# Layer 0's first twelve units: the second product in one piece, behind both pairs of scores and in front of the second tile for the maximum

## The reference, cut to what matters

```python
q = (x @ Wq.T + bq).reshape(b, s, NHEADS, DK)       # 16 heads, width 8, s = 2048
k = (x @ Wk.T + bk).reshape(b, s, NHEADS, DK)
v = (x @ Wv.T + bv).reshape(b, s, NHEADS, DV)
w = jnp.einsum('bshd,bzhd->bhsz', q, k)
w = w / jnp.sqrt(jnp.float32(DV))
w = jax.nn.softmax(w, axis=-1)
vw = jnp.einsum('bhsz,bzhd->bshd', w, v)
out = vw.reshape(b, s, NHEADS * DV) @ Wo.T + bo
```

## Time and profile before

| | us |
|---|---|
| median of 3 runs | 1083.95 (1082.78 to 1086.41) |
| the profiled execution, device time | 1085.42 |
| its span in the profile | 1083.6 |
| PE busy | 1007.7 (93%) |
| DVE busy | 900.6 (83%) |
| ACT busy | 824.1 (76%) |
| POOL busy | 195.8 (18%) |
| mean granted TensorE clock | 0.972 of 2.4 GHz |

### The profile page before, as it was taken

How to read it: one execution, slowest core, us unless ns; L and a number is a source line. 1 busy time by engine, 2 the same in 40 slices (tenths; PEclk the granted TensorE clock), 3 DMA queues, 4 the chain that set the end, 5 groups by cost and what they waited for, 6 DMA issues and landing times.

```text
span 1083.6 us, 22172 instructions
## 1 busy us (share of the span) xinstructions
PE 1007.7 (93%) x8654; PEld 341.6 (32%) x8654; DVE 900.6 (83%) x1153; ACT 824.1 (76%) x1584; POOL 195.8 (18%) x370
## 2 busy tenths in 40 slices
PE   6889999999999999999998899999989998899997
PEld 2422222222222222222232244334344563323323
DVE  8989999999999999999988677766778767897604
ACT  4149999998999998999986577666755676656785
POOL 4533200003000003000024200231042113110112
PEclk9569999999999999999999899999999999999997
DMA  3820511000000000000001441115200431200000
GB/s 98 204 79 7 141 32 26 6 2 2 2 2 2 3 2 2 2 1 3 2 2 31 144 129 51 40 32 94 35 2 9 141 106 37 34 10 1 1 11 11
DMA packets 46422, 41.68 MB, mean 38 GB/s; under 512 B 5598, under 2 KB 44478, under 8 KB 46318
## 3 DMA queue, kind: packets, MB, share of 16 engines
q1 hardware_dynamic: 44062, 34.87, 13.1%
q0 software_dynamic: 1824, 5.25, 1.7%
q10 hardware_dynamic: 432, 0.13, 0.0%
HBM read 26.44 MB, written 13.30 MB: 37 GB/s over the span
## 4 chain that ended last, share of the span: by engine, by line
PE 71%; DVE 13%; ACT 8%; issue 4%; DMA 1%; POOL 1%; another core or an unknown queue 1%; SPq 0%; POOLq 0%; ACTq 0%; DVEq 0%
PE O L989 26%; PE T L957 14%; PE S L917 9%; DVE mx L1280 8%; ACT PT L1527 4%; PE S L924 4%; PE T L966 3%; PE S L1102 2%; PE S L1068 1%; ACT PT L1521 1%; PE S L1058 1%; PE T L1110 1%; PE S L966 1%; PE T L998 1%; PE T L1090 1%
## 5 line engine op out<-in xcount | busy, mean ns | idle before, releaser
L1280 DVE TENSOR_REDUCE mx<-S 128x2 f32<-128x1024 f32 (+2 forms) x672 | 759.3, 1180 | 72.4 <-PE S L917 25.3
L1527 ACT ACTIVATE PT<-T 128x512 f32<-128x512 f32 (+2 forms) x1280 | 675.8, 580 | 116.5 <-PE T L966 49.4
L989 PE MATMUL O<-PT,Va 128*9 128x256 f32 (+1 forms) x4032 | 317.7, 387 | 3.3 <-ACT Os L1562 3.3
L917 PE MATMUL S<-Ks,Qs 48*128 48x512 bf16 x1024 | 205.5, 394 | 12.1 <-DVE mx L1280 9.6
L957 PE MATMUL T<-Qs,Ks 51*128 51x512 bf16 x1024 | 202.0, 387 | 13.4 <-ACT PT L1527 9.3
L957 PEld LDWEIGHTS T<-Qs,Ks 51*128 51x128 bf16 x1024 | 56.2, 93 | 224.1 <-issue 126.7
L989 PEld LDWEIGHTS O<-PT,Va 128*9 128x9 f32 x4032 | 59.8, 88 | 207.1 <-issue 197.5
L924 PE MATMUL S<-K,Qs 96*128 96x512 bf16 (+3 forms) x320 | 89.4, 349 | 5.3 <-DVE mx L1280 4.9
L966 PE MATMUL T<-Qs,K 99*128 99x512 bf16 (+3 forms) x256 | 67.4, 344 | 11.9 <-ACT PT L1527 8.3
L989 PE MATMUL O<-PT,V 128*17 128x512 f32 (+3 forms) x616 | 72.5, 540 | 0.0
L917 PEld LDWEIGHTS S<-Ks,Qs 48*128 48x128 bf16 x1024 | 52.4, 95 | 34.7 <-DVE mx L1280 27.3
(11 more groups left out here) (303 smaller groups left out, 815.3 us busy)
## 6 DMA issues: line engine op xcount, KB each, us to landing
Qs<-in_L_ffn_experts SPq DMA_DIRECT2D x28, 192.0 KB, 2.4
Ks<-in_L_ffn_experts SPq DMA_DIRECT2D x20, 192.0 KB, 2.6
Vf<-sorted_x SPq DMA_DIRECT2D x12, 256.0 KB, 4.8
sorted_y<-Vf SPq DMA_DIRECT2D x12, 256.0 KB, 2.3
Qs<-rows_q SPq DMA_DIRECT2D x24, 128.0 KB, 4.5
rows_q<-q SPq DMA_DIRECT2D x7, 384.0 KB, 2.5
Qs<-rows_q SPq DMA_DIRECT2D x36, 64.0 KB
sorted_x<-XP POOLq DMA_DIRECT2D x1, 1792.0 KB, 10.7
```

Source lines behind the costliest of these rows:

```text
L917: m = e.matmul(two[:, i, :], Qs[r0:r0 + 48, hp, q0:q0 + 128], Ks[r0:r0 + 48, hp, CH * kb:CH * kb + CH], start=True, stop=True, tile_positi ...
L989: m = e.matmul(acc[32 * g:32 * g + d1, lo:hi], v, PT[(2 * j + g // 2) % 4][:, p0 + lo:p0 + hi], start=fresh, stop=True, skip_group_check=n ...
L1280: e.tensor_reduce(mx[:, u % 2, h0:h0 + 2, kb], two[:, :, 0:n], AX.X, ALU.max).then_inc(free, 1)
L1527: e.activation(PT[(2 * j + pair) % 4][:, CH * i + lo:CH * i + CH], bank[:, lo:CH], ACT.Exp).then_inc(free, 1)
```

## The change

In the layer 0 branch of the step loop, for units 0 to 11 (`u < 12`, with u the unit of the scores), the first half of the product is no longer emitted behind the first tile for the maximum, nor the second at the end of the step. The whole product is emitted in one piece right behind the second pair of scores, and the remaining k - 1 tiles for the maximum come behind it. Units 12 to 15 and layer 1 are as before.

```diff
@@ -524,13 +524,18 @@
         emit_st(J, 0)
         if L == 0 and k:
             emit_s()
-            emit_pv(J - LAG, (0,))
+            if u >= 12:
+                emit_pv(J - LAG, (0,))
             do_light(0.5)
             do_later()
             emit_st(J, 1)
+            if u < 12:
+
+                emit_pv(J - LAG, (0, 1))
             for _ in range(k - 1):
                 emit_s()
-            emit_pv(J - LAG, (1,))
+            if u >= 12:
+                emit_pv(J - LAG, (1,))
         else:
             if k:
                 emit_s()
```

## The result

The changed kernel takes 1160.07 us (median of 4 runs, 1158.36 to 1162.89) against 1083.37 for the kernel before beside it: a ratio of 1.0703, interval 1.0685 to 1.0721. The forecast was 1160.

A forecast was written before the change was run, and what follows sets the result against it. PE, DVE and ACT were all taken as full in the first twelve units. Step growth +81.2, copy -3.8, long units -3 and transposes +1.5 gave +76 us on a median of 1083.95: 1160 us, range 1146 to 1173.

The forecast's parts named there:

- The bank chain: Score pairs take two of three banks in turn, so a pair starts at least 1.16 us behind the one before.
- The other three terms, 0.32, 0.98 and 0.22: Rest of the new step: T1 to product 0.32, product to S 0.98, S to next T0 0.22 us.
- The copy's wait, -3.8: A unit's first product no longer waits for ACT's accumulator copy: -0.35 x 11 = -3.8 us.
- The long units, -3: Two units with a chunk's projection and routing: DVE's idle time hides some extra work, -3 us.
- The transposes, +1.5: Transposes between steps now follow an S, whose successor's weights are exposed for 0.1 us: +1.5 us.
- the 0.07 us of waiting: Old step: the chain's 1.16 us exceeds PE's 1.09 us between pairs, costing 0.07 us.
- The main term: Each of 191 steps grows from 2.255 to 2.68 us, by 0.425: +81.2 us.
- Rival 1: Exponential wait does not bite; DVE sets the pace in the twelve units: -6, about 1078 us; chance 0.04.
- Rival 2: PE's short idles make the clock swing: about 1217 us over a fifth of the steps, 1447 over all; chance 0.05.
- Rival 3: The branch is not taken, or T0 to T1 near 0.75 cancels out: no change, 1084 us; chance 0.03.
- reading of the two gaps of before: Old step's half steps: 1.16 us is set by the wait on the exponential, 1.09 by PE's work.
- the signs: Expected in the changed profile: pairs 1.16 and 1.52 us apart, short unit 44.3 us, DVE near 84% busy, clock 1.00.

The follow-up runs named there:

- e5: Changed kernel with the exponential of the first tile of each step's first pair cut to 256 of 512 columns, units 0 to 11: 1129.15 us, ratio 1.0406.
- e4: Changed kernel with both tiles for the maximum in front of the second pair of scores, whole product behind it: 1122.82 us, ratio 1.0348.
- e6: Changed kernel with the maximum taken over 256 of 512 keys in units 1 to 11: 1163.65 us, ratio 1.0725.
- e3: Changed kernel with the whole product between the two pairs, behind the first tile for the maximum: 1156.26 us, ratio 1.0666.
- e7: Kernel before with the first pair's first-tile exponential cut to 256 of 512 columns, units 0 to 11: 1081.24 us, ratio 0.996.
- e11: Changed kernel with PE waiting for the second pair's first bank already in front of the tile for the maximum between the pairs: 1142.29 us, ratio 1.0611.
- e10: Kernel before, units 0 to 11, with PE waiting for the next first pair's first bank before the product's second half: 1079.92 us, ratio 1.0031.
- e1: Changed kernel with the whole product cut into two halves, one right behind the other at the same place: 1163.06 us, ratio 1.0733.
- e9: Kernel before with both tiles for the maximum, second pair, then whole product only in the copy-waiting step of units 1 to 11: 1080.22 us, ratio 1.003.
- e8: e2 with the maximum taken over 256 of 512 keys in units 1 to 11: 1087.1 us, ratio 1.0014.
- e12: Kernel before with e10's early wait in all sixteen units of layer 0: 1078.74 us, ratio 1.0017.
- e2: Changed kernel with halves as before, the first between the pairs, the second in front of the second tile for the maximum: 1096.41 us, ratio 1.0111.

## Why the prediction was right

*The bank chain sets T0 to T1 at 1.16.* Shown: seen at 1.16, moved to 0.94 by a shorter exponential (e5), filled with an S for its full price (e4), not moved by VectorE (e6), and found on the other side when the product is on the other side (e3).

*The other three terms, 0.32, 0.98 and 0.22.* Each as forecast to 0.01 us. 0.32 and 0.98 come from rows of the same instructions in the same order elsewhere in the trace (0.98 with layer 1's S behind the product), 0.22 from T to S, the reverse order. 191 x (2.683 - 2.256) = 81.6, forecast 81.2.

*The copy's wait, -3.8.* Gone in all eleven units.

*The long units, -3.* They are 4.41 us longer than a short one, before 5.47: -2.1 in both together.

*The transposes, +1.5.* Undersized: +3.6. Outside its 16 steps a short unit has 44.41 - 42.93 = 1.48 us; before it had 37.60 - 36.10 = 1.50, of which 0.35 were the copy's wait, so +0.33 a unit. I had counted 0.10 for the accumulator's transposes and nothing for the maxima's, which come behind an S now too. And a gap between pairs with transposes in it has more work than the chain's 1.16, so in the kernel before it did not pay the 0.07 us of waiting that I took off everywhere. The rows, before and then changed, with the accumulator's transposes between the pairs, show 1.67 and 2.21: 0.54 more, where a gap without transposes grew by 0.36 (1.165 to 1.527).

```profile
306.77 0.39 PE L957 MATMUL T<-Qs,Ks 51*128 51x512 bf16 x2
308.44 0.39 PE L957 MATMUL T<-Qs,Ks 51*128 51x512 bf16 x2
```

```profile
344.96 0.39 PE L962 MATMUL T<-Qs,Ks 51*128 51x512 bf16 x2 [0.56 <-ACT PT L1532]
347.17 0.39 PE L962 MATMUL T<-Qs,Ks 51*128 51x512 bf16 x2
```

*What the forecast had no term for.* Unit 0's copy comes 5.2 us later, where its steps should give 6.6 (15 steps at 0.427, and a last product that ends 0.2 us later in its step): -1.4. Some 0.8 of it lies in front of the change, as the first pair comes at 68.22 instead of 69.06 us. And -1.9 behind unit 11, in stages that wait for other work.

Together 81.6 - 3.8 - 2.1 + 3.6 - 1.4 = +77.9 at unit 11, and 76.0 at the end, the difference of the two spans. The main term was right for the reason given. That the total agrees within 1 us is luck: +2.1 for the transposes, +0.9 for the long units and +0.4 for rounding were offset by 3.3 us that the forecast did not have.

*Rival 1, VectorE sets the pace.* Excluded: T0 to T1 would have to be 0.74. *Rival 2, the clock.* The short unit's busy share of PE fell to 35.20 of 44.41, 79% as worked out, and the granted clock stayed at 1.00 from 76 us to 683. The Trainium skill, "TensorE: Matmul & The Clock Gate", section "A second HAM failure mode: psum-queue depth-cycling", says that such short pauses can make the clock swing. In this trace it did not; in the profiles of e4 and e6 single stretches of 3.4 us at 0.50 fell into the twelve units, two and one, so the rival was not empty. *Rival 3.* 191 steps changed as read from the code.

The prediction's reading of the two gaps of before holds: 1.16 is the chain's wait and 1.09 is PE's own work. For the 1.09, e7 shows it (T1 no sooner although its exponential was over 0.30 us before), and e11 shows the chain with one semaphore at 1.07, below it. What the prediction did not know is that the chain's 1.16 holds some 0.09 us for a second semaphore: e11 took it out and T0 to T1 went from 1.156 to 1.067. In e10 the 1.165 could only fall to 1.09, to PE's own work. One number of the signs was off in itself: 16 x 2.68 + 0.7 + 0.6 is 44.2, not 44.3; measured 44.41.

## What to carry to other kernels

Count the buffers between producer and consumer in tiles, and lay out the producer's other work so that each reuse finds its buffer just freed: moving a long operation from between two reuses to behind both opens an empty gap, here 0.72 us a step (1.16 less the two starts of 0.22), and the loss is that gap less the 0.22 us that the merge saved and the 0.07 us that had been waited before. For a new order, look for the same instruction pairs elsewhere in the trace and add up their start-to-start distances; that gave each term of the step here to 0.01 us. The places where the pattern is broken, such as the transposes, want the same care. And when two engines are level, an uneven rhythm for the second one costs even where its total is unchanged.

## What was not expected of the hardware

A second semaphore to wait for in front of a matmul pair cost about 0.09 us where PE was waiting. In e11 T0 to T1 went from 1.156 to 1.067, and the matmul started 0.055 us instead of 0.144 behind the end of its exponential; in e10 1.165 went to 1.09, where PE's own work stops it. In the traces the second wait is a separate instruction in PE's queue.

Two float32 products of 256 columns behind each other took 0.99 us to the next full-width tile, one of 512 took 0.98: the halves cost nothing, only what stands between them.

The granted clock's dips behind the start move with small changes of the code before them. Between the start and the last 20 us of a profile, before has one, at 606.6 us, the changed kernel, e1 and e7 one each, like it some 20 us behind unit 12's copy, e9 and e11 none, e8 and e12 two, e2, e3, e4, e5 and e10 three, e6 four, those of e4 and e6 in part inside the twelve units. In e2, e3 and e10 they are worth 4 to 7 us. What decides it was not tried. For a gain of less than 0.5% in one stage, the stage is to be read on its own, not from the total.
